# Two-layer gated cross-attention: at the head of an iteration, VectorE takes the next queries' statistics behind the first scaling

## The reference, cut to what matters

```python
ln_out = _ln(hidden_states, ln_w, ln_b)
q  = _ln(_fp8_linear_pertensor(ln_out, wq, ...).reshape(b, s, g, hpg, d), ...)   # g = 8 groups, hpg = 2, d = 128
k  = _ln(...); v = ...
core = _gqa(q, k, v)                  # 256 own keys
qx = _ln(_fp8_linear_pertensor(ln_out, wqx, ...).reshape(b, s, g, hpg, d), ...)
kx = _ln(...); vx = ...               # from the context
xout = _gqa(qx, kx, vx)               # 1601 cross keys
return einsum(_div_clamp_fp8(concatenate([core, xout])), wproj) * ...
```

## Time and profile before

| | |
|---|---|
| median of 3 runs | 1675.88 us (1675.58 to 1676.2) |
| the profiled execution | 1677.2 us, its span 1675.4 us |
| PE, DVE, ACT, POOL busy | 95%, 83%, 83%, 68% of the span |
| granted TensorE clock | 0.99 of full |
| layer 0's attention loop | from about 60 us to 1150 us of the span |

### The profile page before, as it was taken

One profiled execution on the slowest core, in us unless ns is written; L12 is line 12 of the kernel. 1 busy time (PEld: TensorE's weight loads), 2 busy tenths in 40 slices (PEclk: granted clock), 3 DMA queues, 4 the chain that ended last, 5 costly groups with the idle time before them and its releaser, 6 DMA issues. The chain is left out here.

```text
span 1675.4 us, 44071 instructions
## 1 busy us (share of the span) xinstructions
PE 1596.8 (95%) x15996; PEld 1002.3 (60%) x15996; DVE 1388.3 (83%) x3486; ACT 1388.2 (83%) x2346; POOL 1140.8 (68%) x1775
## 2 busy tenths in 40 slices
PE   3799999999999999999999999998998999999998
PEld 2476777767777677777777777776554333333333
DVE  7899999999999989999988999898896755655422
ACT  6688888888887888888888888786347999999997
POOL 3668778687787777888788888876675655646300
PEclk9899999999999999999999999998999999999999
DMA  4399989899988998999999999999323222222100
GB/s 179 90 198 205 195 195 197 188 209 210 203 194 200 217 207 187 217 223 215 210 193 212 210 210 207 196 194 250 100 51 111 46 56 69 42 38 47 33 14 14
DMA packets 609481, 261.12 MB, mean 156 GB/s; under 512 B 576624, under 2 KB 581744, under 8 KB 607856
## 3 DMA queue, kind: packets, MB, share of 16 engines
q1 hardware_dynamic: 605040, 258.05, 71.7%
q10 hardware_dynamic: 4224, 0.25, 0.2%
HBM read 99.15 MB, written 17.29 MB: 70 GB/s over the span
## 5 line engine op out<-in xcount | busy, mean ns | idle before, releaser
L1816 PE MATMUL score<-KK,QT 128*128 128x512 bf16 (+2 forms) x1920 | 341.6, 322 | 7.6 <-DVE mxp L1299 6.9
L1836 PE MATMUL pv<-PT,VV 128*128 128x256 bf16 (+1 forms) x2880 | 339.5, 274 | 9.7 <-DMA PT<-PB 9.6
L1570 ACT ACTIVATE PB<-S,rsum 128x1024 bf16<-128x1024 f32 (+1 forms) x256 | 246.3, 988 | 114.0 <-DVE rsum L1330 84.8
L1836 PEld LDWEIGHTS pv<-PT,VV 128*128 128x128 bf16 (+1 forms) x2880 | 280.1, 98 | 76.7 <-issue 36.1
L1321 DVE SCALAR_TENSOR_TENSOR PB<-S,rsum,PB 128x1024 bf16<-128x1024 f32 (+1 forms) x256 | 291.9, 1141 | 2.6 <-ACT PB L1570 2.6
L1816 PEld LDWEIGHTS score<-KK,QT 128*128 128x128 bf16 x1920 | 157.4, 98 | 146.2 <-DVE mxp L1299 15.8
L1560 ACT ACTIVATE S<-S,nmx 128x1601 f32<-128x1601 f32 x128 | 210.2, 1642 | 6.0 <-DVE nmx L1311 5.9
L2887 ACT ACTIVATE P<-score 128x1024 f32<-128x1024 f32 x196 | 197.7, 1052 | 1.7 <-PE score L2979 0.8
L2999 PE MATMUL pv<-P,V 128*9 128x256 f32 (+1 forms) x2288 | 152.6, 380 | 1.1 <-DVE pv L2270 0.8
L1128 POOL TENSOR_SCALAR S<-S,rsum 128x256 f32<-128x256 f32 x128 | 74.9, 585 | 115.2 <-DVE rsum L1330 101.4
L1695 PE MATMUL tb<-stage,wsb 128*128 128x512 bf16 (+1 forms) x768 | 149.2, 337 | 4.3 <-DVE stage L645 3.9
(11 more groups left out here) (295 smaller groups left out, 3665.6 us busy)
## 6 DMA issues: line engine op xcount, KB each, us to landing
x<-rs_d SPq DMA_DIRECT2D x16, 936.0 KB, 5.2
rsb<-rs_d SPq DMA_DIRECT2D x16, 936.0 KB, 5.4
wsb<-w_split SPq DMA_DIRECT2D x46, 256.0 KB, 4.6
wsb<-w_split SPq DMA_DIRECT2D x23, 512.0 KB, 5.2
wpr<-in_wprojT SPq DMA_DIRECT2D x23, 512.0 KB, 6.6
context_d<-stage SPq DMA_DIRECT2D x16, 400.2 KB, 4.0
l_ctx<-context_d SPq DMA_DIRECT2D x4, 1601.0 KB, 7.6
rawh<-in_w_all SPq DMA_DIRECT2D x12, 512.0 KB, 5.6
```

Source lines behind the costliest of these rows:

```text
L1570: e.activation(m.PB[n % 2][:, 2 * a:a + b], m.S32[n % 2][:, a:b], ACT.Copy, scale=m.rsum[n % 2][:, 1:2]).then_inc(s["p_hi"], 1)
L1816: i = e.matmul(m.score[:, at:at + b - a], qt[:, kind, qp, q * P:(q + 1) * P], kk[:, kp, a:b], start=(k == 0), stop=(k == 2))
L1836: i = e.matmul(m.pv[:, at:at + 256], vv[0:rows, v, t, :], m.PT[k % 2][0:rows, turned(c, a), :], start=(c == first and r == 0), stop=(c == ...
```

## The change

In DVE's order, `query_stats(it + 1, 0)` moves from the iteration's very head to behind `scaled(4 * it, 0)`. In front of the pair stands `invert(4it - 1)`, behind it `p_lo(4it - 1, 0)`; in iteration -1 `scaled` does nothing, and from iteration 31 on `query_stats` does nothing. No instruction, wait or transfer is added or taken away.

```diff
@@ -1356,10 +1356,10 @@
     for it in range(-1, NGB + LAG - 1):
-        query_stats(it + 1, 0)
         if it == NGB:
             dve_turned_low(e, m, s, 0)
         scaled(4 * it, 0)
+        query_stats(it + 1, 0)
         p_lo(4 * it - 1, 0)
         keys_low(it + 1, 0)
```

## The result

The changed kernel takes 1708.49 us (median of 5 runs, 1705.66 to 1710.2) against 1676.2 us (1675.58 to 1676.47) for the kernel before on the same chip: the ratio is 1.0189, 95% interval 1.0178 to 1.0199. That is 32.3 us slower; 19.4 were worked out, and the time lies at the very end of the range (1682 to 1708), half a microsecond past it. The profiled execution's span is 1706.8 us, 31.4 more than before, and all of it arises in layer 0's attention.

A forecast was written before the change was run, and what follows sets the result against it. It took iterations 3 to 11 as bound by a hand-over loop (PE, ScalarE, DVE, `mxp`), 12 to 14 by DVE, 15 on by PE; terms 11.8 + 2.1 + 1.9 + 0.4 + 0.7 + 1.0 + 1.5 = 19.4 gave 1695.3 us, range 1682 to 1708.

The forecast's parts named there:

- The gap at the scaling: DVE at the head: scaling directly behind the reciprocal starts after 0.17 us idle, 0.24 us more on everything there.
- the port lock: POOL beside DVE's PB1: L1086 takes 1.14 us instead of 0.20; aggregation to norm 2.88 against 2.37, 0.51 us more.
- the norm's line: Statistics, POOL's norm, ScalarE's `kn`, PE's turn: the norm comes 1.12 + 0.24 + 0.51 = 1.87 us later.
- the wait at the turn: PE at L1780, iterations 3 to 11: waits about 1.6 us for `kn`, the turn 1.18 us late.
- case (c): Rival: POOL's last norm instruction L1091 falls behind the next subtraction, 18 us more, 1713 us; chance 0.07.
- its price in 3 to 11: Iterations 3 to 11 lose 1.18 us each through the late turn, 10.6 us of the forecast's sum.
- The wait for `mxp` at the head: PE's wait before scores 4it+1 in iterations 3 to 11 disappears, as `mxp` comes 0.9 to 1.2 us earlier.
- case (a): Rival: the line through `kn` is hidden, only the wait for `mxp` goes, 1670 us; chance 0.06.
- the pricing of the iterations behind 11: Attention iterations 12 to 14: 0.7 us; 16 to 24: 0.06 each, 0.5 for 20; 25 to 30: 0.25 each.
- wait of DVE for POOL's `PB`: DVE's scaling of 4it+1 (L1299) waits some 1.5 us for POOL's split (L1132), costed at nothing.
- 1.18 us on every iteration: Iterations 3 to 11 and 15: iteration 5's late turn repeats anew, even ones the same; 10 x 1.18 = 11.8 us.

The follow-up runs named there:

- ninth: Changed kernel with TensorE's keys(it+1, 2) moved ahead of turn_queries(it+1, 0), so PE works while `kn` is late: 1702.90 us (1.0152).
- twelfth version: Changed kernel with POOL's `catq` writing 8 of its 512 columns from the fifth pair on, that computation left out: 1702.21 us (1.0159).
- tenth version: Kernel before, with the statistics behind the scaling in iterations 3 to 11 only and keys(it+1, 2) ahead of turn_queries(it+1, 0) in all: 1684.31 us (1.0041).
- third version: Kernel before, with the statistics moved behind the scaling in iterations 3 to 11 only: 1690.60 us (1.0089).
- eighth version: Changed kernel with PB2, DVE's second low part of block 4it-1, ahead of the scaling of the own keys: 1728.66 us (1.0310).
- sixth: Changed kernel with DVE's low part of the first keys placed between the statistics and the first low part of block 4it-1: 1710.95 us (1.0204).

## Why the forecast was right in direction and short in size

**Right, step by step.** The gap at the scaling (0.17 us idle in 22 of the iterations 2 to 30, 0.22 to 0.68 in 13, 15, 16 and 21 to 24), the port lock (1.14 us; aggregation to norm 2.88 us instead of 2.37, from iteration 3 on), their sum on the norm's line (r + 3.73 to r + 5.64, 1.91 us against 1.87), the wait at the turn (1.06 us in even and 1.77 us in odd iterations of 3 to 11, 1.96 in 7), L1091 just ahead of the next subtraction (0.15 us, against 0.18 worked out; so not case (c)), and its price in 3 to 11 (11.05 us against 10.6). The wait for `mxp` at the head went, and nothing was gained by it, since PE waits at the turn instead: case (a) is out. Iteration 15 cost 1.4 us against 1.2, 21 to 24 0.5 against 0.2, 0 to 2 5.6 against 4.4; in iteration 1 a fall of the clock behind PE's wait of 1.96 us at the turn is in it (the iteration loses 2.86 us, and 0.66 and 0.93 in the ninth and twelfth version, where the clock held; these versions differ in other ways too):

```profile
103.00:104.00 1.00, 0.00 (x0) 1.00 1.15 222
104.00:105.00 1.00, 0.34 (x2) 0.78 1.11 211
105.00:106.00 1.00, 0.78 (x5) 0.50 0.19 39
106.00:107.00 1.00, 1.00 (x5) 0.50 0.33 69
107.00:108.00 1.00, 1.00 (x8) 0.52 1.22 142
```

**The step that failed** is the pricing of the iterations behind 11: "DVE is full and PE's lateness disappears in PE's waits for DVE; the 0.24 us stays: 0.7" for 12 to 14, 0.06 each in 17 to 19 (0.5 in 20), and 0.25 each in 25 to 30. Measured are 2.35, 5.29 (16 to 20) and 6.35 us: 14.0 where the terms gave 2.9, so that these 11.1 us are nearly all of the 13 that lack. Two things were missed there.

First, the port was read in one direction only: POOL behind DVE, and never DVE behind POOL. Moving the norm's end to r + 5.64 put `catq`, which starts at r + 5.59, on the start of PB2. In the kernel before `catq` ran beside scalings that read PSUM and met nothing; iteration 26 before, and after:

```profile
961.04 1.15 POOL L1150 TENSOR_TENSOR catq<-yt,ym 128x512 bf16<-128x512 f32 x1
...
962.68 0.88 DVE L1321 SCALAR_TENSOR_TENSOR PB<-S,rsum,PB 128x640 bf16<-128x640 f32 x1
```

```profile
990.25 1.15 POOL L1150 TENSOR_TENSOR catq<-yt,ym 128x512 bf16<-128x512 f32 x1
...
990.25 1.83 DVE L1321 SCALAR_TENSOR_TENSOR PB<-S,rsum,PB 128x640 bf16<-128x640 f32 x1
```

That is 0.95 us of DVE's time in each iteration from 3 to 30 (PB2 0.88 before, 1.83 after), except 25, where it is 0.64. With the gap's 0.24 it is 1.19, and 26 and 27 take 1.20 us more each. That this fits so well is partly luck: other VectorE instructions, L1350 and its two followers above all, fall longer or shorter beside POOL in these two iterations, by up to 1.0 us each way, and nearly cancel. In 17 to 20 DVE has no idle time, but for the gap, from the head to the scaling of 4it+1, which comes at r + 10.30 instead of r + 9.33, and PE, which waited for nothing in iteration 17 before, waits twice:

```profile
677.92 0.63 PE L1780 MATMUL pa<-ident,kn 128*128 128x128 f32 x4 [0.33 <-ACT kn L1514]
...
682.16 1.47 PE L1816 MATMUL score<-KK,QT 128*128 128x512 bf16 x6 [0.34 <-DVE mxp L1299]
```

The same collision explains a check of the forecast that failed: no wait of DVE for POOL's `PB` showed at 4it+1, since the longer PB2 filled that time. The rule of the Trainium skill that the forecast used (SBUF — State Buffer, Who interferes with whom) names no preferred side: the first to issue keeps the pair. The traces agree both ways, L1086 1.14 us instead of 0.20 behind DVE, PB2 1.83 us instead of 0.88 behind POOL.

Second, the late norm was taken to act through PE alone. It also holds ScalarE, and through the squares, the keys and the values DVE: taking PE's wait away (9) or DVE's stretch away (12) left most of the loss in its place. In iteration 26 the two lines are 0.2 us apart (35.60 and 35.38), so neither cure alone can give much there; for the other iterations this is argued and not shown. Of the 11.1 us, taking `catq` away gave 3.6 back in 12 to 14, 16 to 20 and 25 to 30.

In 3 to 11 the sum came out right partly by luck. The forecast put 1.18 us on every iteration, from PE's wait in iteration 5, and said that the even ones come to the same. Measured are 0.88 in the odd ones and 1.5 in the even ones, where the path is ScalarE's and not PE's, and filling PE's wait gave 1.1 us back in all nine.

**Open.** Both cures at once were not tried, so it isn't shown that with the gap, `catq` and the late norm all gone nothing is left. A run with a shorter norm line, which would have measured the norm's share in 17 to 20 and 25 to 28 by itself, wasn't made either. In iteration 28, which loses 1.68 us where 26 and 27 lose 1.20, the two L1350 take 1.17 and 0.90 us instead of 0.63 and 0.33; in iteration 20 of the tenth version, which loses 2.0 us, L677 takes 2.51 us instead of 1.05. These too are VectorE instructions stretched while POOL works, in places that no experiment chose: shifts of the order by tenths of a microsecond change which of them meet, and no run tells these chance meetings from the change's own.

## What to carry to other kernels

When an instruction moves, move everything that it releases on the timeline too, and lay the new times of *both* engines that share a port over each other: a neighbour that starts in the same 0.1 us can cost a whole instruction, on either side. Price a late result by every engine that stands in order behind it, not by the one on which the first wait shows; where a second line is 0.2 us behind the first, no single cure pays. And a wait of TensorE can cost more than its idle time, when the granted clock falls behind it: count the falls in each trace before two versions are compared.

## What was unexpected of the hardware

- TensorE's granted clock fell to its 1.2 GHz level behind single waits of 1.95 us for `kn` (iterations 7 and 8 of the third version, 5 of the twelfth, 1 of the changed kernel), each time for 3.4 us, 1.7 us of clock. The wait's length doesn't tell whether it falls: it fell behind one of 1.75 us (iteration 27 of the eighth version), and not behind 1.96 us (7 of the changed kernel), 2.04 (5 of the sixth) or 2.49 (8 of the eighth). The same iteration with and without a fall differed by 1.3 to 2.9 us.
- A GpSimd instruction of 0.20 us on 128 x 4 elements is stretched to 1.14 us by one of 1.25 us on VectorE, and the power of 1.02 us to 2.06: the losses, 0.94 and 1.04 us, are near what the other still had to run (1.07 and 1.19 us).
- Where `catq` and PB2 start in the same instant, GpSimd had the port: PB2 takes 1.83 or 1.84 us in 28 of the iterations 1 to 30, all but 1 and 25, in which it starts at another time than `catq`.
- The scaling, with four waits ahead of it, starts behind 0.17 us of idle time where it follows a 0.15 us instruction; with three of the waits issued ahead of that instruction, 0.19 us of idle time stood before it instead.
